# Layer norms behind self-attention: which engine copies the turned rows, and how the shift column is formed

## What is computed

```python
h = ctx @ Wo + bo + hidden_states
mu = jnp.mean(h, axis=-1, keepdims=True)
var = jnp.mean(jnp.square(h - mu), axis=-1, keepdims=True)
out = (h - mu) * jax.lax.rsqrt(var + EPS) * ln_gamma + ln_beta
...
x = _layernorm(x + out, axis=-1)
```

## Time and profile before

| | us |
|---|---|
| median of three executions | 4018.85 (4017.84 to 4019.07) |
| the profiled execution, its own time | 4019.18 |
| its span in the trace | 4017.5 |
| time outside of the span | 1.7 |
| this stage, from its first instruction to the next stage's first transfer | 1911 to 2127, some 216 |

### The profile page before, as it was taken

One profiled execution on the slowest core, in us unless ns is written; L12 is line 12 of the kernel. 1 busy time (PEld: TensorE's weight loads), 2 busy tenths in 40 slices (PEclk: granted clock), 3 DMA queues, 4 the chain that ended last, 5 costly groups with the idle time before them and its releaser, 6 DMA issues. The chain is left out here.

```text
span 4017.5 us, 65629 instructions
## 1 busy us (share of the span) xinstructions
PE 3610.5 (90%) x19584; PEld 2245.6 (56%) x19584; DVE 2185.1 (54%) x5904; ACT 1752.4 (44%) x3767; POOL 1859.9 (46%) x1684
## 2 busy tenths in 40 slices
PE   6999989999999999998677999999799978887686
PEld 4777767777677777776234555555455532121253
DVE  4666656666566666666685666666333321111255
ACT  3666656666566666664234555555121210000033
POOL 2666656656566666665435777777311000000112
PEclk9999999999999999999898999999999989889798
DMA  6999999999899999997553232222454339999523
GB/s 251 392 385 382 378 356 374 384 381 381 334 386 393 379 384 383 388 382 305 158 169 125 82 92 83 85 85 74 146 178 149 110 146 418 422 421 420 216 96 113
DMA packets 412983, 1083.60 MB, mean 270 GB/s; under 512 B 24672, under 2 KB 90848, under 8 KB 363488
## 3 DMA queue, kind: packets, MB, share of 16 engines
q1 hardware_dynamic: 395472, 1032.01, 68.4%
q10 hardware_dynamic: 16656, 47.19, 3.0%
q0 software_dynamic: 512, 0.26, 0.0%
HBM read 642.64 MB, written 436.73 MB: 269 GB/s over the span
## 5 line engine op out<-in xcount | busy, mean ns | idle before, releaser
L530 POOL TENSOR_SCALAR a_sc<-a_sc,a_inv 128x512 f32<-128x512 f32 x512 | 823.4, 1608 | 586.4 <-DVE a_inv L473 541.9
L482 DVE COPY a_pt<-a_ps_t 128x512 f32<-128x512 f32 x512 | 353.5, 690 | 546.5 <-PE a_ps_t L216 529.2
L1076 POOL TENSOR_SCALAR b_sc<-b_sc,b_inv 128x128 f32<-128x128 f32 (+3 forms) x512 | 546.8, 1085 | 189.2 <-DVE b_inv L1045 185.9
L352 ACT ACTIVATE a_stage_q<-a_ps_b 128x640 f32<-128x640 f32 x512 | 360.8, 705 | 588.4 <-PE a_ps_b L232 553.3
L1006 ACT ACTIVATE b_sc<-b_sc,b_mx 128x128 f32<-128x128 f32 (+3 forms) x512 | 281.9, 551 | 322.2 <-DVE b_mx L1039 322.0
L466 DVE CUSTOM_DVE_ANT_0 a_sc<-a_ps_s,a_rq 128x512 f32<-128x512 f32 x512 | 353.1, 690 | 75.3 <-PE a_ps_s L206 60.0
L342 ACT ACTIVATE a_sc<-a_sc,a_mx 128x512 f32<-128x512 f32 x512 | 370.0, 723 | 54.8 <-DVE a_mx L466 50.7
L352 ACT ACTIVATE a_stage_k<-a_ps_b 128x640 f32<-128x640 f32 x512 | 357.4, 698 | 0.0
L216 PEld LDWEIGHTS a_ps_t<-a_ident,a_sc 128*128 128x128 f32 x2048 | 247.6, 141 | 146.5 <-issue 141.0
L1039 DVE CUSTOM_DVE_ANT_0 b_sc<-b_ps_s,b_mask 128x128 f32<-128x128 f32 (+3 forms) x512 | 229.3, 488 | 168.4 <-PE b_ps_s L954 164.5
L1595 PE MATMUL d_ps_y<-d_w,d_prod 128*8 128x512 f32 x512 | 255.1, 662 | 70.3 <-DMA d_w<-in_e_W 66.5
(11 more groups left out here) (205 smaller groups left out, 6360.3 us busy)
## 6 DMA issues: line engine op xcount, KB each, us to landing
band_q<-a_stage_q SPq DMA_DIRECT2D x128, 1280.0 KB, 7.1
band_k<-a_stage_k SPq DMA_DIRECT2D x128, 1280.0 KB, 10.2
a_rk<-band_k SPq DMA_DIRECT2D x128, 1024.0 KB, 12.7
a_rq<-band_q SPq DMA_DIRECT2D x256, 512.0 KB, 13.5
d_w<-in_e_W SPq DMA_DIRECT2D x32, 4096.0 KB, 37.1
d_wg<-in_e_Wg SPq DMA_DIRECT2D x16, 4096.0 KB, 28.1
a_okv<-in_b_wkv ACTq DMA_DIRECT2D x62, 512.0 KB, 7.9
k<-a_kv SPq DMA_DIRECT2D x64, 256.0 KB, 10.9
```

The lines of the kernel that those rows point to most:

```text
L352: act.activation(st[h % 2][:, t, :], src, ACT.Copy).then_inc(sem[f"a_{kind}_staged"], 1)
L482: dve.tensor_copy(pt[:, h % 2, :, t * P:(t + 1) * P], ps_t[:, :].rearrange("p (r n) -> p r n", r=T4)).then_inc(sem["a_pt_out"], 1)
L530: pool.tensor_scalar(sc[n][:, :], sc[n][:, :], inv[:, n:n + 1], None, ALU.mult)\
L1076: pool.tensor_scalar(sc[j % 2][i][:, 0:width(i)], sc[j % 2][i][:, 0:width(i)], inv[j % 2][:, i:i + 1], None, ALU.mult).then_inc(sem["b_nor ...
```

## The change

- `turned_out` leaves DVE's loop, where it was the last part of a step, and becomes the first part of ACT's step, with the same two waits. The copy is now an activation `Copy`. Its unit in step `s` is still `s - 5`.
- In `scales`, the one operation that gave the shift column (mean times -1 times the inverse) becomes two: `0 - mean` into column 11, then that times the inverse into column 10. The zero is a new 128 x 1 tile, filled once. Both norms use `scales`.

```diff
+        zero = sb("zero", [P, 1])
...
                 dve.reciprocal(s_[:, r, 9:10], s_[:, r, 8:9]).then_inc(sem[f"{z}inv{r}"], 1)
-                dve.wait_ge(sem[f"{z}inv{r}"], u + 1)
-                dve.scalar_tensor_tensor(s_[:, r, 10:11], s_[:, r, 6:7], -1.0, s_[:, r, 9:10], ALU.mult, ALU.mult)\
+                dve.tensor_tensor(s_[:, r, 11:12], zero[:, :], s_[:, r, 6:7], ALU.subtract).then_inc(sem[f"{z}inv{r}"], 1)
+                dve.wait_ge(sem[f"{z}inv{r}"], 2 * u + 2)
+                dve.tensor_tensor(s_[:, r, 10:11], s_[:, r, 11:12], s_[:, r, 9:10], ALU.mult)\
                    .then_inc(sem[f"{z}scales{r}"], 1)
...
-            def turned_out(u, j):
-                dve.wait_ge(sem[z + "turned"], u + 1)
-                dve.wait_ge(sem[f"{z}stored{j}"], (u - j) * (32 // R) + 32)
-                dve.tensor_copy(yT[j][:, :, :], ps_y[j % 2][:, :].rearrange("p (k n) -> p k n", k=K4))\
-                   .then_inc(sem[z + "yT"], 1)
...
-                if has(s, OUT):
-                    turned_out(s - OUT, (j - OUT) % R)
-
+
+            dve.memset(zero[:, :], 0.0).then_inc(sem[z + "zero"], 1)
+            dve.wait_ge(sem[z + "zero"], 1)
...
+            def turned_out(u, j):
+                act.wait_ge(sem[z + "turned"], u + 1)
+                act.wait_ge(sem[f"{z}stored{j}"], (u - j) * (32 // R) + 32)
+                act.activation(yT[j][:, :, :], ps_y[j % 2][:, :].rearrange("p (k n) -> p k n", k=K4), ACT.Copy)\
+                   .then_inc(sem[z + "yT"], 1)
+
             def step(s, j):
+                if has(s, OUT):
+                    turned_out(s - OUT, (j - OUT) % R)
```

More of the change, by code:

```diff
@@ L810, in norm_sems @@
     return [z + n for n in ["sp_waited", "pool_waited", "dve_waited", "const_in", "projected", "biased", "biased_h", "y", "yT",
-                            "summed", "turned", "shifted", "scaled", "normed", "eps", "bn0", "bn1",
+                            "summed", "turned", "shifted", "scaled", "zero", "normed", "eps", "bn0", "bn1",
                             "var0", "var1", "std0", "std1", "inv0", "inv1", "scales0", "scales1"]
```

## The result

Over 20 executions each, the changed kernel takes 4026.41 us (median, 4014.97 to 4041.27) and the kernel before 4018.23 (4010.25 to 4023.07). The ratio is 1.0024, with a 95% interval of 1.0014 to 1.0033: slower by a quarter of a per cent. The prediction was 4027.0, inside a range of 4004 to 4046. The spread is itself a result: the changed kernel's executions lie 26 us apart, those of the kernel before 13.

The account below looks back on a forecast made before the run. DVE was taken as the fullest engine, losing time in operations held by POOL or behind PE; steady +3.8, fill +2, drain -0.6 and disturbance +3 gave +8.2 us, a median of 4027.0, range 4004 to 4046.

Parts of the forecast that it names:

- DVE's own step: DVE's loop step without stalls: from 5.22 us to 4.81, the copy gone and the column operations added.
- PE's bound: Loop from column through norm, turn and projection to `add`: a step is at least 5.09 us, before 4.48.
- POOL's phase: When POOL's two sums (a pair) meet DVE: they start 5.2 us after a copy's end, 0 to 1.5 behind S.
- S: The start of `add` on DVE; a step runs from one S to the next.
- the law: Steady loop: POOL's pair stalls the first norm's columns, two steps sum to 12.27 us, a step is 6.14.
- all that disturbs: Steady loop: extra from longer steps where the second norm's columns are met, over before's 9.5 us: +3 (-5 to +12).
- lock-in: Rival: POOL's pair holds both second-norm columns, mean step 7.3 us, PE's clock low, 4040 to 4055; chance 0.15.
- Steady: 24 steps at 6.14 plus 5.09 give 152.5 us where 148.7 were measured before: +3.8.
- fill: Start of the stage, POOL working without a pause: two more column operations for each of two steps can wait, +2 us.
- drain: End of the stage, POOL done: three steps at 0.41 less, last copies on ACT +0.6, in all -0.6 us.
- PE's loop as the bound: Rival: POOL's pairs no longer meet DVE's two-input operations, step 5.09 us, total 3999; chance 0.18.
- The draw: Rival: late loads or SP held elsewhere, saved work and stalls cancel, step 5.8 to 6.0, 4014 to 4019; chance 0.13.

Follow-up runs that it names:

- the two runs where the stalls are gone and the turn has its old place: Changed kernel with POOL's sums cut to 8 of 512 columns: 0.9936; changed kernel with a one-tensor-input column and POOL's pair held back by a wait: 0.9938.
- first profile: Profile of one of the changed kernel's longer executions in its first set, 4036.46 us; that set's ratio against the kernel before is 1.0024.
- second profile: Later profile of the unaltered changed kernel, execution of 4022.07 us; ratio of that measurement against the kernel before 1.0015.
- the copy alone: Kernel before with only the copy moved to ACT, the shift column still one operation: 0.9992 against the kernel before.
- columns-only kernel: Kernel before with only the shift column made by two operations, the copy still on DVE: 1.0030 against the kernel before.
- the two runs with one norm each: Kernel before with two column operations in one norm and one tensor_scalar in the other: first norm 0.9995, second norm 1.0004.
- second set of executions: The unaltered changed kernel timed again, 12 executions: median 4021.87 us, ratio 1.0015 against the kernel before.
- the one-tensor column: Changed kernel with the shift column as one tensor_scalar, its mean the only tensor input: 0.9988 against the kernel before.
- the kernel with the late turn: Changed kernel with one-tensor-input column and POOL's pair held back by a wait, plus PE's turn, ACT's copy and SP's stores one step later: 0.9929.

## Why the prediction came out right, point by point

- **What bounds.** Right. DVE's operations hide the lost time, and POOL causes it. This was inferred from 64 column operations with a mean of 357 ns and from the fill; cutting POOL's sums, and gating them at full size, showed it.
- **The cost of the parts.** DVE's own step was to be 4.81: undisturbed steps of the changed kernel are 4.73 to 4.78. PE's bound was to be 5.09: the mean step is 5.00 and 4.97 in the two runs where the stalls are gone and the turn has its old place. Copy on ACT 0.60: 0.58. Both new columns were to be well over 0.16: they are 0.38 each, the first under the 0.5 to 1 named for it.
- **POOL's phase.** From a copy's end to POOL's pair were to be 5.2 us: 5.27 on average over 24 in the first profile. In the second profile the pairs start at S - 0.4 to S + 1.2, where 0 to 1.5 was named. The copy mostly ends at S + 1.2 to S + 1.4, not at S + 1.56, so pairs came 0.2 to 0.4 sooner than the law had them. Since a pair that comes sooner holds DVE for less, the step is shorter: 5.95, not 6.14, in the second profile, and 5.77, not 6.02, with the copy alone. Where the old column is held by POOL's first operation, gamma's product can also slip in between POOL's two, which the law charged in full.
- **The two columns of the second norm.** Here the term was too small. The forecast had +3 us for all that disturbs, and gave lock-in 0.15. The first profile is lock-in in every second step, with a mean of 6.68 (7.3 was named for it). It is not an exception: executions of the changed kernel lie from 4015 to 4041. In the columns-only kernel, for which the law said 5.72, it looks like the rule (a step of 6.41, and all ten executions between 4025 and 4033). What the law missed is PE, which the forecast named for the lock-in and for before's late steps, but left out of the law. A long step leaves PE idle (4.27 us in the example), the granted clock is low behind it, and the late projection makes the next step long as well, 6.8 where the rival had it shrink to 5.1. The law counts ACT's copy from S, at S + 1.56, but the copy follows DVE's last column; when DVE then waits 2 us for PE, the copy ends ahead of S and POOL's pair comes at S + 4.2 to S + 5.5 again. No run changes the clock by itself, so how much of this chain hangs on it rests on the rows above. In the first profile DVE waits 24 us for PE behind the first three sums; before it was 6.6.
- **The sum.** Steady +3.8, fill +2, drain -0.6, disturbance +3: +8.2. (The sum at 1957.95, from which it counts 25 steps, is the seventh and not the sixth; the count is right.) In the second profile the steady stretch is +0.1, the fill +3.4, the drain -1.8; the stage is +1.7. In the first they are +18.3, +3.8 and -1.8, and the stage is +20.3. That the fill's extra comes from the first norm's pair of operations is seen in the two runs with one norm each: 32.4 us from the first sum to the seventh with the two operations in the first norm, 30.1 with them in the second, 29.9 before. The median lies between the two profiled executions; how the others divide was not profiled. That the total came out at 8.2 is luck in good part: steady stretch and disturbance were to be +6.8 together and were +0.1 and +18.3, and the second set of executions has the changed kernel 4.7 us over before by the medians. The sign, the stalls of the first norm's columns and the fill's extra came as forecast.
- **The rivals.** PE's loop as the bound was seen as soon as POOL's sums were cut or gated, never with the pairs left free. The draw is what the second profile looks like in its step (5.95), though not by the cause named for it: from copy to pair are 5.29 us there.

## What to carry to other kernels

Look for operations on DVE that read two tensors from SBUF while POOL works, however small: a 128 x 1 operation of 0.16 us can wait for a whole operation of another engine, and two of them in a row can wait twice. Give one of the operands as a scalar pointer and the operation isn't held (0.21 to 0.22 us in each of 128 cases, 46 of them wholly inside a POOL operation). When work is taken off the bounding engine, ask which transfers its semaphore releases and where the work behind them will now fall; here one extra wait on POOL, which places its pair where DVE has nothing to share, was worth about 20 us with the one-tensor column (0.9938 against 0.9988) and nothing with the two operations (1.0029), while the copy's move alone gave a change that the measurement can't tell from none.

## What the runs showed of the hardware that had not been expected

POOL and DVE do not always take turns. The forecast took from the fill that the one in waiting goes next. In the kernel with the late turn one gamma product found a POOL operation under way and was passed over by four more; timelines of DVE and POOL:

```profile
1937.05 1.25 POOL L715 TENSOR_TENSOR na_xg<-na_x,na_beta 128x512 f32<-128x512 f32 x1
...
1937.62 6.13 DVE L753 TENSOR_TENSOR na_h<-na_h,na_gamma 128x512 f32<-128x512 f32 x1
...
1938.28 1.25 POOL L712 TENSOR_TENSOR na_xb<-na_x,na_bo 128x512 f32<-128x512 f32 x1
1939.50 1.26 POOL L715 TENSOR_TENSOR na_xg<-na_x,na_beta 128x512 f32<-128x512 f32 x1
1940.72 1.25 POOL L712 TENSOR_TENSOR na_xb<-na_x,na_bo 128x512 f32<-128x512 f32 x1
1941.94 1.25 POOL L715 TENSOR_TENSOR na_xg<-na_x,na_beta 128x512 f32<-128x512 f32 x1
```

It began at 1937.62 and took 6.13 us, to 1943.75, just behind POOL's last operation of its backlog. In the copy-only kernel one column operation took 4.46 us in the same way. In six other profiles the longest gamma product of the fill took 1.83 or 1.84. What decides between the two was not tried. So behind a backlog on POOL the bound of one operation, which the prediction used, doesn't hold.
